# A four-layer transformer kernel: in its last stage the first chunk's norm moves in among the output projections, and VectorE takes over the scaling of the last sum

## What is computed

```python
def _layernorm(x, axis=-1, eps=1e-05):
    m = jnp.mean(x, axis=axis, keepdims=True)
    v = jnp.var(x, axis=axis, keepdims=True)
    return (x - m) / jnp.sqrt(v + eps)
...
x = x + _layernorm(_L1_attn_ref(_layernorm(x, axis=-1), ...), axis=-1)
x = x + _layernorm(_L1_ffn_ref(_layernorm(x, axis=-1), L1_ffn_W0, L1_ffn_bias0, L1_ffn_W1, L1_ffn_bias1), axis=-1)
```

```python
X = x.reshape(-1, H).astype(jnp.float16)
D = jnp.dot(X.astype(jnp.float32), W0.T) + bias0          # 256 -> 1024
D = jax.nn.gelu(D, approximate=False).astype(jnp.float16)
E = jnp.dot(D.astype(jnp.float32), W1.T) + bias1          # 1024 -> 256
return E.astype(jnp.float16).reshape(B, L, H)
```

## Time and profile before

| what | value |
|---|---|
| median of 3 timed runs | 1359.48 us (1359.06 to 1362.21) |
| the profiled execution's own time | 1354.88 us |
| its span, from first to last instruction | 1353.1 us |
| TensorE matmul busy | 1159.4 us (86%) |
| VectorE / ScalarE / GpSimd busy | 855.6 (63%) / 620.5 (46%) / 362.0 us (27%) |
| mean granted TensorE clock | 0.921 |
| last stage, first instruction to the span's end | 1243.8 to 1353.1 us |

### The profile page before, as it was taken

One profiled execution on the slowest core, in us unless ns is written; L12 is line 12 of the kernel. 1 busy time (PEld: TensorE's weight loads), 2 busy tenths in 40 slices (PEclk: granted clock), 3 DMA queues, 4 the chain that ended last, 5 costly groups with the idle time before them and its releaser, 6 DMA issues. The chain is left out here.

```text
span 1353.1 us, 25314 instructions
## 1 busy us (share of the span) xinstructions
PE 1159.4 (86%) x9088; PEld 966.7 (71%) x9088; DVE 855.6 (63%) x2162; ACT 620.5 (46%) x1420; POOL 362.0 (27%) x460
## 2 busy tenths in 40 slices
PE   6669997347599988677789999999999999999895
PEld 5546775345498977555558888888888888888775
DVE  6467896727566656587365666666666666664474
ACT  5434554112144432467644554554454445553564
POOL 3321231375401437583042014002400240000110
PEclk9779998558899998887899999999999999999898
DMA  6648874121399764253243233223342332221001
GB/s 176 180 120 221 231 204 169 58 101 65 107 360 401 271 246 126 79 183 135 86 119 102 79 102 118 78 79 105 115 140 84 108 107 82 83 86 67 1 17 47
DMA packets 77961, 177.21 MB, mean 131 GB/s; under 512 B 12614, under 2 KB 26182, under 8 KB 75270
## 3 DMA queue, kind: packets, MB, share of 16 engines
q1 hardware_dynamic: 71564, 158.54, 36.2%
q0 software_dynamic: 6272, 17.05, 4.2%
HBM read 114.26 MB, written 61.08 MB: 130 GB/s over the span
## 5 line engine op out<-in xcount | busy, mean ns | idle before, releaser
L2300 ACT ACTIVATE decay<-masked,negcum 128x128 f32<-128x128 f32 x512 | 164.0, 391 | 240.7 <-issue 156.1
L2216 PE MATMUL joint<-xh,w_high 128*128 128x512 f32 x512 | 211.7, 413 | 1.7 <-POOL wl L2157 1.7
L2216 PE MATMUL joint<-xh,wl 128*128 128x512 f32 x512 | 200.6, 392 | 0.0
L2405 DVE COPY cT<-joint 128x512 f32<-128x512 f32 x128 | 88.4, 691 | 176.3 <-PE joint L2216 176.3
L2216 PE MATMUL joint<-xl,w_high 128*128 128x512 f32 x512 | 199.7, 390 | 0.0
L2227 PEld LDWEIGHTS pcb<-cT,bT 128*128 128x128 f32 x1024 | 134.5, 191 | 10.6
L2227 PE MATMUL pcb<-cT,bT 128*128 128x128 f32 x1024 | 135.3, 275 | 0.0
L2154 POOL TENSOR_TENSOR w_high<-w_in,none 128x512 fp32r<-128x512 f32 x32 | 34.6, 1083 | 319.5 <-DMA w_in<-in_w_bc 319.4
L2216 PEld LDWEIGHTS joint<-xh,w_high 128*128 128x128 f32 x512 | 96.5, 188 | 22.5 <-issue 4.8
L2216 PEld LDWEIGHTS joint<-xh,wl 128*128 128x128 f32 x512 | 96.1, 188 | 21.1
L2216 PEld LDWEIGHTS joint<-xl,w_high 128*128 128x128 f32 x512 | 96.6, 189 | 15.3
(11 more groups left out here) (377 smaller groups left out, 2702.9 us busy)
## 6 DMA issues: line engine op xcount, KB each, us to landing
cumrow<-ssm_cum SPq DMA_DIRECT2D x128, 256.0 KB, 3.3
slots_in<-blank SPq DMA_DIRECT2D x16, 1024.0 KB, 5.4
rows<-slots_in SPq DMA_DIRECT2D x32, 512.0 KB, 5.3
slots_out<-spare SPq DMA_DIRECT2D x32, 512.0 KB, 3.7
weights<-in_expert_quads SPq DMA_DIRECT2D x16, 768.0 KB, 9.2
w_in<-in_w_bc SPq DMA_DIRECT2D x32, 256.0 KB, 3.6
qk_parts<-parts SPq DMA_DIRECT2D x32, 192.0 KB
stack<-qk_parts SPq DMA_DIRECT2D x32, 192.0 KB, 5.3
```

What stands on the lines that cost most here:

```text
L2216: last = nc.tensor.matmul(bank[:], w[:, j, col:col + P], a[:, k, c * CHUNK:(c + 1) * CHUNK], start=(m == 0), stop=(m == len(parts) - 1))
L2300: last = nc.scalar.activation(decay[:, n % 2, o], masked[:, n % 2, o], ACT.Exp, bias=negcum[:, c * TPC + i, head:head + 1])
L2405: nc.vector.tensor_copy(cT[:, n % 2, :], pcT[:]).then_inc(c_out, 1)
```

## The change

The normalisation of both sums into x goes over to the middle stage's form: VectorE adds y times the deviation's inverse in one scalar_tensor_tensor for each tile, as soon as the power is done, without the shift. The shift of LN_Y is the same for a whole row, so LN_X doesn't see it; it is added with that of LN_END at the end, in one ScalarE pass (`finish`). The statistics use bn_aggr. The perceptron's output stays in float16 (`y16`) and isn't cast back. The first chunk's norm, sum, statistics and turning move in among the projections; in the chunks the order behind the casts and gelus changes. A store covers two tiles.

```diff
-        order = [(LN_Y, 0), (LN_Y, 1), (LN_X, 0)]
+        order = [(LN_Y, 0), (LN_X, 0), (LN_Y, 1)]
         for g in range(NCH):
-            order += [(LN_Y, g + 2)] * (g + 2 < NCH) + [(LN_END, g - 1)] * (g > 0) + [(LN_X, g + 1)] * (g + 1 < NCH)
+            order += [(LN_X, g + 1)] * (g + 1 < NCH) + [(LN_Y, g + 2)] * (g + 2 < NCH) + [(LN_END, g - 1)] * (g > 0)
...
-                for g in range(NCH):
-                    sp.wait_ge(x_final, g + 1)
-                    sp.dma_start(ins["out"][:, tiles(g), :], x[:, tiles(g), :]).then_inc(stored, 16)
+                for b in range(NCH * PAIRS_C):
+                    sp.wait_ge(x_final, b + 1)
+                    sp.dma_start(ins["out"][:, 2 * b:2 * b + 2, :], x[:, 2 * b:2 * b + 2, :]).then_inc(stored, 16)
...
+                    nc.gpsimd.tensor_tensor(rstd[:, kind, tiles(g)], norms["var"][:, kind, tiles(g)], power[:], ALU.pow
+                                            ).then_inc(rstd_ready, 1)
+                    pool.wait_ge(rstd_ready, n)
+                    last = nc.gpsimd.tensor_tensor(shift[:, kind, tiles(g)], norms["negmean"][:, kind, tiles(g)],
+                                                   rstd[:, kind, tiles(g)], ALU.mult)
+                    if kind == LN_END:
+                        link(last)
+                        last = nc.gpsimd.tensor_tensor(shift[:, kind, tiles(g)], shift[:, kind, tiles(g)],
+                                                       shift[:, LN_Y, tiles(g)], ALU.add)
+                    last.then_inc(shift_ready, 1)
...
                 for b in range(JOINT, NCH * PAIRS_C):
+                    if b == NCH * PAIRS_C - 1:
+                        turn(0)
                     project(b)
-                turn(0)
...
+                def finish(b):
+                    act.wait_ge(shift_ready, until(LN_END, b // PAIRS_C))
+                    for i in (2 * b, 2 * b + 1):
+                        act.wait_ge(end_added, i + 1)
+                        last = nc.scalar.activation(x[:, i, :], x[:, i, :], ACT.Identity, bias=shift[:, LN_END, i:i + 1])
+                    last.then_inc(x_final, 1)
...
-                    if n in (2, NFH - 1):
-                        take(JOINT + n // (NFH - 1))
-                for half in range(2):
-                    scale_y(LN_Y, 0, half, y_scaled)
-                for b in range(JOINT + 2, NCH * PAIRS_C):
-                    take(b)
+                    if n in (2, 5):
+                        take(JOINT + n // 5)
                 for b in range(PAIRS_C):
-                    normal(b)
+                    normal_rows(b)
+                    take(JOINT + 2 + b)
                 for b in range(PAIRS_C):
                     high_part(b)
+                take(NCH * PAIRS_C - 1)
...
-                        if n in (0, 1) and g + 1 < NCH:
-                            scale_y(LN_Y, g + 1, n, y_scaled)
-                        if n in (3, 4) and g:
-                            scale_y(LN_END, g - 1, n - 3, end_scaled)
-                        if n in (5, 6) and g + 1 < NCH:
-                            normal((g + 1) * PAIRS_C + n - 5)
+                        if n in (3, 4) and g + 1 < NCH:
+                            normal_rows((g + 1) * PAIRS_C + n - 3)
+                        if n in (5, 6) and g:
+                            finish((g - 1) * PAIRS_C + n - 5)
...
+                def add(g):
+                    dve.wait_ge(rstd_ready, until(LN_Y, g))
+                    for i in range(g * TPC, (g + 1) * TPC):
+                        last = nc.vector.scalar_tensor_tensor(x[:, i, :], y[:, i, :], rstd[:, LN_Y, i:i + 1],
+                                                              x[:, i, :], ALU.mult, ALU.add)
+                    link(last)
+                    statistics(rows_of(x, g), LN_X, g)
+
+                def end(g):
+                    statistics([y16[:, i, :] for i in range(TPC)], LN_END, g)
+
+                def add_end(g):
+                    dve.wait_ge(rstd_ready, until(LN_END, g))
+                    for i in range(TPC):
+                        m = g * TPC + i
+                        nc.vector.scalar_tensor_tensor(x[:, m, :], y16[:, i, :], rstd[:, LN_END, m:m + 1], x[:, m, :],
+                                                       ALU.mult, ALU.add).then_inc(end_added, 1)
...
-                    link(nc.vector.tensor_copy(y[:, tiles(g), :], y16[:]))
...
+                of_y(0)
+                for n in range(2):
+                    low(n)
+                add(0)
+                for n in range(2, NFH):
+                    low(n)
                 of_y(1)
-                link(add(0, y_scaled))
-                statistics(x, LN_X, 0)
...
                         hidden(g, n)
-                        if n == 0 and g + 2 < NCH:
+                        if n == 0 and g + 1 < NCH:
+                            add(g + 1)
+                        if n == 1 and g + 2 < NCH:
                             of_y(g + 2)
-                        if n == 1 and g:
-                            statistics(y, LN_END, g - 1)
-                        if n == 2 and g + 1 < NCH:
-                            link(add(g + 1, y_scaled))
-                        if n == 3 and g + 1 < NCH:
-                            statistics(x, LN_X, g + 1)
-                        if n == 6 and g:
-                            add(g - 1, end_scaled).then_inc(x_final, 1)
+                        if n == 2 and g:
+                            end(g - 1)
+                        if n == 4 and g:
+                            add_end(g - 1)
                     leave(g)
-                statistics(y, LN_END, NCH - 1)
-                add(NCH - 1, end_scaled).then_inc(x_final, 1)
+                end(NCH - 1)
+                add_end(NCH - 1)
```

More of the change, by code:

```diff
@@ L2440, in stage_back @@
         y16 = sb("y16", [P, TPC, D], F16)
[L2441 to L2444, removed]
+        norms = {n: sb("norm_" + n, shape) for n, shape in (
+            ("stats", [P, BACK_KINDS, NT, 6]), ("moments", [P, BACK_KINDS, NT, 2]), ("power", [P, TPC]),
+            ("negmean", [P, BACK_KINDS, NT]), ("var", [P, BACK_KINDS, NT]), ("rstd", [P, BACK_KINDS, NT]),
+            ("shift", [P, BACK_KINDS, NT]))}
+        power, rstd, shift = norms["power"], norms["rstd"], norms["shift"]
         xn16 = sb("xn16", [P, 2, 2, D], F16)
@@ L2454, in stage_back @@
         chain, pool_link = chip.sem("norm_chain"), chip.sem("pool_link")
-        var_ready, rstd_ready = chip.sem("var_ready"), chip.sem("rstd_ready")
-        y_scaled, end_scaled = chip.sem("y_scaled"), chip.sem("end_scaled")
+        var_ready, rstd_ready, shift_ready = chip.sem("var_ready"), chip.sem("rstd_ready"), chip.sem("shift_ready")
+        end_added = chip.sem("end_added")
         xn_rounded, xn_ready, xn_turned, hi_ready = (chip.sem(n) for n in ("xn_rounded", "xn_ready", "xn_turned",
@@ L2481, in _ @@
                 sp.dma_start(bias1[:], ins["ffn_b1"]).then_inc(loaded, 16)
-                for g in range(NCH):
-                    sp.wait_ge(x_final, g + 1)
-                    sp.dma_start(ins["out"][:, tiles(g), :], x[:, tiles(g), :]).then_inc(stored, 16)
-                sp.wait_ge(stored, NCH * 16)
+                for b in range(NCH * PAIRS_C):
+                    sp.wait_ge(x_final, b + 1)
+                    sp.dma_start(ins["out"][:, 2 * b:2 * b + 2, :], x[:, 2 * b:2 * b + 2, :]).then_inc(stored, 16)
+                sp.wait_ge(stored, NCH * PAIRS_C * 16)
             @block.gpsimd
@@ L2492, in _ @@
                 for kind, g in order:
[L2493 to L2496, removed]
+                    n = until(kind, g)
+                    pool.wait_ge(var_ready, n)
+                    nc.gpsimd.tensor_tensor(rstd[:, kind, tiles(g)], norms["var"][:, kind, tiles(g)], power[:], ALU.pow
[8 more added lines that the diff above has]
+                    last.then_inc(shift_ready, 1)
             @block.tensor
@@ L2560, in take, with normal_rows @@
                     nc.scalar.activation(flat(y[:, 2 * b:2 * b + 2, :]), bank_of(b)[:], ACT.Copy).then_inc(y_in, 1)
[L2562 to L2573, removed]
+                def finish(b):
[4 more added lines that the diff above has]
+                    last.then_inc(x_final, 1)
+                def normal_rows(b):
+                    act.wait_ge(shift_ready, until(LN_X, b // PAIRS_C))
                     if b >= 2:
                         act.wait_ge(xn_turned, b - 1)
-                    scaled(xn16[:, b % 2, 0, :], x[:, 2 * b, :], LN_X, 2 * b)
-                    scaled(xn16[:, b % 2, 1, :], x[:, 2 * b + 1, :], LN_X, 2 * b + 1).then_inc(xn_rounded, 1)
+                    normal(nc, norms, xn16[:, b % 2, 0, :], x[:, 2 * b, :], LN_X, 2 * b)
+                    normal(nc, norms, xn16[:, b % 2, 1, :], x[:, 2 * b + 1, :], LN_X, 2 * b + 1).then_inc(xn_rounded, 1)
                     act.wait_ge(xn_rounded, b + 1)
@@ L2620, in _ @@
                             high_part(b)
-                for half in range(2):
```

(17 more changed lines are left out.)

## The result

The changed kernel takes 1350.2 us, median of 6 runs (1347.9 to 1355.3), against 1359.3 for the kernel before on the same chips; the ratio is 0.9937 with a 95% interval of 0.9908 to 0.9966. In a later set of 7 runs it took 1349.7 against 1359.7, ratio 0.9914 (0.9885 to 0.9943). The forecast was 1349.6.

The account below looks back on a forecast made before the run. TensorE lacking work at the last stage's entry, inside its chunks and in its serial tail was the bound; entry 6.0, chunks -0.9 + 1.4 + 0.85, tail 2.0, stores 0.5 make 9.85 us off 1359.48: 1349.6 us, range 1346 to 1354.5.

Parts of the forecast that it names:

- The sum: Whole last stage: 6.0 - 0.9 + 1.4 + 0.85 + 2.0 + 0.5 = 9.85 us gained.
- Entry: Last stage's start: first chunk's norm and turning done among the projections; third up projection 6.0 us earlier (worst 5.5).
- the rival in which the third up waits for the splits: Last stage's start: gain never arrives, splits or bias loads delay the third up projection; 3.9 us or less; chance 0.08.
- Chunks: Chunks 0 to 3: 1.6 us idle before second down projection, waits for turned rows gone; -0.9, +1.4, +0.85, 0 us.
- Tail: After the last matmul, bias sum to last shift: 7.25 us against 9.2, gain 2.0 us (1.5 to 2.4).
- the two POOL shifts: After the last power: ScalarE's shifts need two POOL operations, slowed beside VectorE's sums, taken as 1.0 us.
- the rule that I had set beside it: Kernel's end: each POOL shift waits out a 0.48 us VectorE sum, 1.44 for 1.0 us, gain 1.5.
- Stores: Span's end: half the bytes left behind the last shift, the other pair issued 0.8 before; gain 0.5 us (0 to 0.7).
- the wait at the head of each chunk: Chunk starts: rival that VectorE holds TensorE up by more than 1.6 us, gain 4.1 to 7.5 us; chance 0.24.
- the slower case: Chunks: rival that new gaps drop TensorE's clock from 2.4 to 1.2 GHz, 1364 us, slower than before; chance 0.03.

Follow-up runs that it names:

- the split: The changed kernel with statistics of the sum moved behind VectorE's second cast and those of y behind its fourth; last stage 96.66 us against 99.5.
- the longer block: The changed kernel with eight more unused statistics, 2.7 us, on VectorE behind the sum's statistics in chunks 0 to 2; last stage 111.83 us against 99.5.
- the run with one store: The changed kernel with one store of 512 KB a chunk again; last stage 100.08 us, 0.59 more than with the change.
- the early table: The changed kernel with a one-column gelu ahead of ScalarE's last take of a projection, loading the table earlier; last stage 97.89 us, 1.60 less.

## Why the prediction was right

*Method.* Counting durations from the last stage alone and setting the gain against the median, not against the profiled time, was what carried it: the first profile of the change is not faster than that of before at all.

*The sum.* That it came within 0.1 us is luck in part: the chunks gave 0.6 less than I had and the tail, the entry and the store 0.3, 0.1 and 0.1 more. So is the median, 0.6 from my figure, where one kernel's runs span 7 us.

*Entry, 6.0 forecast, 6.09.* The first up came at 18.71 in the stage; I had 1262.9, which is 19.05 in it. The third up came at 22.2, as I had it, by two errors that cancel: the first up was 0.34 earlier, since I had counted from the end of the last projection, which overlaps the next matmul by that much (1269.45 + 3.62 against 1272.72), and from first to third up it took 3.49 for my 3.2, as the table load began only 1.36 us behind the first up (1272.72 to 1274.08) and not 1.13. ScalarE began to normalise at 10.45 in the stage, where I had 10.55 (1254.4), and the power beside the splits took 1.38 for my 1.34. The split weights were done at 12.2, 6.5 us ahead of the first up, so the rival in which the third up waits for the splits had nothing to stand on.

*Chunks, +1.35 forecast, +0.72.* The mechanism held, and the split and the longer block show it from both sides. The size was off by 0.2 us a chunk. I took a late cast as lost start-to-start time only; but the first matmul after a wait also takes longer to give way (0.23 us to the start of the next 256-column one, 1280.68 to 1280.91, against 0.12 between the later ones), so each bracketed wait of 0.19 to 0.21 costs 0.47 and each of 1.5 about 1.76, counted from start to start against the spacing without a wait. Chunk 1 has three such restarts: some 2.75 us over the 15.9 of work, where I had 2.6.

*Tail, 2.0 forecast, 2.34.* The term that was mis-sized is the two POOL shifts. I took 1.0 us for them from the middle stage's 0.44 beside VectorE's sums; they took 0.61 (1348.69 to 1349.30), 0.20 and 0.25 of it in the operations, although VectorE summed from SBUF at that very time. By the rule that I had set beside it, of the Trainium skill's page SBUF — State Buffer (Who interferes with whom), the two would have taken 1.44; the trace does not show that here. In chunk 2 the same two POOL operations took 0.41 and 0.32 us while VectorE ran a cast and sums of the same kind; what decides between them I have not tried.

*Stores, 0.5 forecast, 0.6,* and shown by the run with one store.

*The rivals.* VectorE did become the wait at the head of each chunk, at the forecast size. The clock did not fall behind waits of 1.5 us, three in each of four profiles with the change's chunks (the change twice, the early table, the single store), and fell each time around one of 4.1 us. So the mechanism of the slower case is real; where between these it begins was not sought.

## What to carry to other kernels

When a stage is short against the kernel's scatter, compare the stage by its own first and last instruction: here two profiles of one kernel gave it as 99.49 and 99.52 us while its totals scattered by several. An in-order engine that feeds another should have its side work in pieces shorter than what the fed engine has queued: the same work in one piece of 3.7 us cost 2.8 us more over three chunks than in pieces of 1.7 and 2.0. Look behind the last work of one kind for the first of the next (norm, turning, table load): if it can go in one step earlier, the wait goes, and in this entry the slower clock behind it went too.

## What was not expected

The stages ahead, with the same instructions in all ten profiles, delivered the last stage at any time from 1243.85 to 1254.44 us. The spread is there in the first copies of the expert stage (428.4 to 437.4) and grows to 555.8 to 567.5 at the first sum of the middle stage; the stage in question repeated as 99.49 and 99.52. I have not looked for the cause.

The price of a late VectorE block is not linear. A first wait of 1.5 us cost 1.8; 2.7 us of VectorE work more cost 3.8 to 4.4 a chunk, since the clock then goes to 1.2 GHz, for 3.4 us in chunks 0 and 2 and for 6.8 in chunk 1, of which 5.7 are work.
